# Feature products split over the rows of the array: two half-height products per half of the columns, instead of one full-height product

## The reference, cut to what matters

```python
# block 1, per batch; x is the group-normed input
S = softmax(V_s . sigmoid(prod2 + b_s))           # (N, N), spatial attention
for k in range(3):
    r = einsum('mn,bmn,bmft->bnft', cheb[k], S, x)
    out = out + einsum('bnft,fo->bnot', r, Theta[k])
sg = relu(out)
tc = conv(sg, tw, kernel 1x3 over time) + tb
y = layer_norm(relu(einsum('bnft,of->bnot', x, rw) + rb + tc))
# block 2: gate -> softmax -> top 2 of 8 experts -> gelu(x w1) * (x w3) -> w2
```

## Time and profile before

| | us |
|---|---|
| median of 3 runs | 697.05 (696.73 to 697.25) |
| the profiled execution's own time | 696.03 |
| its span | 694.0 |
| PE busy | 555.2 (80%) |
| DVE busy | 409.3 (59%) |
| ACT busy | 251.8 (36%) |
| POOL busy | 213.7 (31%) |

### The profile page before, as it was taken

How to read it: one execution, slowest core, us unless ns; L and a number is a source line. 1 busy time by engine, 2 the same in 40 slices (tenths; PEclk the granted TensorE clock), 3 DMA queues, 4 the chain that set the end, 5 groups by cost and what they waited for, 6 DMA issues and landing times. The chain is left out here.

```text
span 694.0 us, 12572 instructions
## 1 busy us (share of the span) xinstructions
PE 555.2 (80%) x2488; PEld 362.5 (52%) x2489; DVE 409.3 (59%) x1809; ACT 251.8 (36%) x619; POOL 213.7 (31%) x283
## 2 busy tenths in 40 slices
PE   0567599999999999999985225999999999999243
PEld 0233357766666666666663102666666666665122
DVE  4645236888888888988889771333333333332255
ACT  0343144345544444445442110333333333333232
POOL 5000001224333444443345440334334433443100
PEclk9989599999999999999999556999999999999655
DMA  9900000000000000000001032222222222221597
GB/s 299 421 4 1 0 1 1 0 1 32 31 30 30 31 30 30 30 23 23 27 27 55 31 106 70 77 85 83 84 85 91 78 85 87 91 83 42 164 321 240
DMA packets 36247, 52.69 MB, mean 76 GB/s; under 512 B 4606, under 2 KB 31361, under 8 KB 35969
## 3 DMA queue, kind: packets, MB, share of 16 engines
q1 hardware_dynamic: 24816, 30.86, 14.3%
q0 software_dynamic: 6480, 16.85, 6.5%
q10 hardware_dynamic: 4928, 4.72, 2.1%
HBM read 30.19 MB, written 23.14 MB: 77 GB/s over the span
## 5 line engine op out<-in xcount | busy, mean ns | idle before, releaser
L619 PE MATMUL bank<-w,xT 128*128 x284 | 135.9, 601 | 2.1 <-DVE xT L1420 2.1
L1420 DVE COPY xT<-bank 128x256 f32<-128x256 f32 x71 | 30.2, 425 | 143.8 <-PE bank L606 143.8
L975 POOL DMA_INDIRECT yrows<-xT,dest x71 | 69.4, 978 | 139.4 <-ACT xT L831 135.3
L496 PE MATMUL bank<-work 128*128 128x256 f32 x384 | 93.3, 386 | 0.0
L944 POOL DMA_INDIRECT xrows<-xtok,slot x64 | 64.3, 1005 | 81.4 <-DVEq L1315 66.7
L932 POOL TENSOR_TENSOR yg<-work,sml 128x512 f32<-128x512 f32 x16 | 18.0, 1122 | 196.3 <-DVE work L1225 193.0
L496 PEld LDWEIGHTS bank<-work 128*128 128x128 f32 x384 | 70.4, 190 | 9.0 <-issue 0.8
L634 PE MATMUL bank<-w,xT 128*128 x284 | 73.3, 380 | 1.6 <-ACT xT L836 1.6
L619 PEld LDWEIGHTS bank<-w,xT 128*128 128x128 f32 x284 | 48.8, 192 | 37.6 <-issue 37.6
L825 ACT ACTIVATE xT<-bank 128x256 f32<-128x256 f32 x71 | 27.4, 386 | 94.9 <-PE bank L619 94.9
L634 PEld LDWEIGHTS bank<-w,xT 128*128 128x128 f32 x284 | 48.5, 190 | 6.2 <-issue 2.6
(11 more groups left out here) (203 smaller groups left out, 1017.9 us busy)
## 6 DMA issues: line engine op xcount, KB each, us to landing
xT<-xrows SPq DMA_DIRECT2D x71, 129.0 KB
xT<-yrows SPq DMA_DIRECT2D x32, 256.0 KB, 3.9
xs<-x_in SPq DMA_DIRECT2D x4, 1024.0 KB, 10.8
w<-w13t_in SPq DMA_DIRECT2D x1, 4096.0 KB, 18.3
out<-xT ACTq DMA_DIRECT2D x16, 256.0 KB, 3.7
w<-w2t_in SPq DMA_DIRECT2D x1, 2048.0 KB, 22.7
yrows<-xT,dest POOLq DMA_INDIRECT x71, 2.4
xrows<-xtok,slot POOLq DMA_INDIRECT x64
```

The lines of the kernel that those rows point to most:

```text
L496: last = mm(bank[6][:, h * N:(h + 1) * N], z[:, p, c, k, h], A[:, p, c, k], start=(c == 0 and k == 0), stop=(c == C - 1 and k == K - 1))
L619: last = mm(bank[2 + q][:, :], xc[:, q, c], w13[:, e, c].rearrange("p w n -> p (w n)"), start=(c == 0), stop=(c == C - 1))
L975: pool.indirect_dma_start(yrows, bass.IndirectOffsetOnAxis(ap=dest[:, q], axis=0), yo[:, q], None, bounds_check=2 * TOKENS - 1, oob_is_err ...
L1420: V.tensor_copy(xc[:, q].rearrange("p c k -> p (c k)"), bank[q][:, 0:C * P]).then_inc(c_xc, 1)
```

## The change

One call of `features` now makes four products of 64 rows by 192 columns, where it made two of 128 rows by 384 columns. Row half r holds the time steps 4r to 4r+3 of each h. Since `thetabd` is block-diagonal, rows 0 to 63 have something only in the columns of their own four time steps, and so have rows 64 to 127: the products left out are those with blocks of zeros. Row half r of both h goes into `bank[4 + r]`, h = 0 into its first 192 columns and h = 1 into the next. ACT's two copies per call are now one per r, of 384 columns each as before, and write to `z` in runs of 64. A call now waits once for both copies of the call before it, and `b_z` is raised once per bank, after the h = 1 product.

```diff
             def features(b, p, c):

                 pe.wait_ge(s["b_xb"], done(b))
+                pe.wait_ge(s["b_zc"], (b * 4 + c * 2) + START)
                 for h in range(H):
-                    pe.wait_ge(s["b_zc"], (b * 4 + (c * H + h)) + (START - 1))
-                    mm(bank[4 + h][:, 0:K * P], xTb[:, p, h, c * P:(c + 1) * P],
-                       thetabd[:].rearrange("p k t o -> p (k t o)"), start=True, stop=True).then_inc(s["b_z"], 1)
+                    for r in range(2):
+                        rows = slice(r * P // 2, (r + 1) * P // 2)
+                        last = mm(bank[4 + r][:, h * K * P // 2:(h + 1) * K * P // 2], xTb[rows, p, h, c * P:(c + 1) * P],
+                                  thetabd[rows, :, r * TH // 2:(r + 1) * TH // 2].rearrange("p k t o -> p k (t o)"),
+                                  start=True, stop=True)
+                        if h == H - 1:
+                            last.then_inc(s["b_z"], 1)
...
             def copy_features(b, p, c):
-                for h in range(H):
-                    act.wait_ge(s["b_z"], (b * 4 + (c * H + h + 1)) + START)
-                    nc.scalar.copy(z[:, p, c, :, h], bank[4 + h][:, 0:K * P].rearrange("p (k o) -> p k o", k=K)
+                for r in range(2):
+                    act.wait_ge(s["b_z"], (b * 4 + (c * 2 + r + 1)) + START)
+                    nc.scalar.copy(z[:, p, c, :, :, r * P // 2:(r + 1) * P // 2],
+                                   bank[4 + r][:, 0:K * P].rearrange("p (h k o) -> p k h o", h=H, k=K)
                                    ).then_inc(s["b_zc"], 1)
```

## The result

The changed kernel takes 706.24 us (median of 4 runs, 704.71 to 707.76), the one before 697.15 in the same rounds: 1.0114 times as long, 95% interval 1.0084 to 1.0143. (The two medians by themselves give 1.0130.) It is slower by 1.1%, where 0.12% faster was forecast. The profiled execution took 707.76 us, with a span of 705.7.

The account below looks back on a forecast made before the run. PE was taken to bound turns -1 to 1 and DVE's chain turns 3 and later. Changes of -0.24, -0.29 and -0.29 us sum to -0.8, so 697.05 becomes 696.2 us, range 694.9 to 698.9.

Parts of the forecast that it names:

- What bounds which turn: PE sets turns -1 to 1; DVE's own chain sets turns 3 and later, with PE waiting 0.16 or 0.38 us before `prefix`.
- The halves side by side, a call of 0.86: In `features`: eight MATMULs overlap in five steps (0.81 us), paced by weight loads to 0.86, 0.43 less; chance 55%.
- The switches: Changing array shape around `features` costs 0.19 us each: one new for a c=0 call, two for c=1.
- -0.29: Forecast change of turn 1, and of turn 0, in us: -0.24 for the c=0 call and -0.05 for c=1.
- -0.8: Forecast change of turns -1 to 1 together, in us: -0.24, -0.29 and -0.29.
- The merged wait, the copies: Waiting for both copies of the call before costs 0; ACT's copies take 0 to 0.1 us more each, covered.
- The step that failed: From turn 3 on, a faster `features` only lengthens PE's wait before `prefix`, worth nothing.
- the sum: Adds the changes of turns -1 to 1 to -0.8 us, all coming through, and nothing from turn 3 on.
- my rivals: For `features` calls: full halving 695.2 us, 12%; second loads not hidden 698.5, 14%; halves one after another 699.3, 15%.
- the remainder of 4%: Chance of something outside, such as a copy that slows or a clock edge falling otherwise behind the stage.
- My sign of being wrong: If turns 3 and later change in length, the forecast is wrong, for then DVE isn't their bound.
- the gain is eaten: In `features`: once a call's eight MATMULs take over some 1.1 us, the switches eat the gain.

Follow-up runs that it names:

- run 1: Changed kernel plus three spare full-height products ahead of `prefix` in turns 3 to 14: 697.96 us against 697.19 before.
- Run 2: Kernel before, full-height products, from batch 5 on 256 (c=0) or 312 (c=1) of the 384 `features` columns: 706.99 us, ratio 1.0135.
- run 9: Changed kernel with both products of each h taken from rows 0 to 63: 705.21 us, a single execution.
- runs 3: Half-height form for batches 0 to 2 alone (made in turns -1 to 1), the old form for the rest: 697.90 us, ratio 1.0013.
- run 7: Changed kernel with three spare products in turns 3 to 14, more in turns -2, -1, 15 to 18 and ahead of the first expert tile: 692.37 us, ratio 0.9919.
- run 4: Changed kernel with a call's four products reordered, both h of row half 0 first, then both of row half 1: 705.97 us, ratio 1.0133.
- run 5: Changed kernel plus one spare full-height product ahead of `prefix` in turns 3 to 14: 705.83 us, ratio 1.0109.
- run 10: Changed kernel plus two spare full-height products ahead of `prefix` in turns 3 to 14: 701.06 us, a single execution.
- run 11: Changed kernel plus six spare products of 64 rows ahead of `prefix`, instead of three of 128 rows: 698.32 us, a single execution.

## Why the prediction was wrong

*What bounds which turn:* right. PE sets turns -1 to 1, and from turn 3 on the time saved in `features` appeared as a longer wait ahead of `prefix` (3.5 to 12.2 us).

*The halves side by side, a call of 0.86:* the time is right, its making only in part. There are four steps of 0.162 and not five; with one bare load and the switch at its end they also come to 0.86. That already holds the switch out of the call, which I had added once more for c=1.

*The switches:* mis-sized; I had put them at 0.19 each. Into a call it costs 0.09 (the six MATMULs of `graph` ahead of it take 118.62 - 117.23 = 1.39 in place of 1.30), and the exposed load behind it another 0.10 (125.28 - 123.45 = 1.83 in place of 1.73 for the next `logits`). Turn 1 gained 0.69 us where -0.29 was forecast; turns -1 to 1 together 1.9 in run 1 where -0.8 was.

*The merged wait, the copies:* right, they cost nothing: the two copies take 0.86 after as before 0.84 to 0.96, and DVE's wait for `product` in turn 1 is 1.38, where it was 1.82.

*The step that failed* stands in its first part: "a faster `features` only makes PE wait longer", and at the end of the sum: "From turn 3 on nothing." I priced PE's idle time at zero because DVE sets the pace. But PE's clock hangs on it. With 1.0 to 1.3 us ahead of `prefix` in place of 0.16 to 0.38, beside the 0.95 ahead of `tokens`, the clock fell seven times in ten turns, and at the worst place: within or just behind `tokens`, with `logits` next, and DVE does wait for these. DVE's waits for `gn_mean`, `gn_var` and `logits` grow from 2.4 to 9.0 us. Turns 4 to 13 took 8.3 us more, where the sum had nothing. Run 2 shows it without the change, run 1 by filling only the idle time. What picks the turns in which the clock falls, and why it fell in run 9 with less idle time than before, stays open. None of my rivals had this mechanism; the remainder of 4% named a clock edge, but behind the stage. The page of the profile did hold what I should have asked: the granted clock was 1.00 in every turn although PE waited over 1 us in each, and where a level holds, the question is how near its edge the kernel stands. The Trainium skill, page "TensorE: Matmul & The Clock Gate", section "Why this matters for your kernels", warns of long idle gaps between bursts of matmuls; this case shows that shorter ones can do it too: in turns 4 to 13 no gap was over 1.3 us, with five small products between the two of a turn, and they cost the clock in seven of ten turns.

*My sign of being wrong,* that turns 3 and later change in length, came true from turn 4 on: 18.4 to 19.2 us and more; turn 3 stayed, 17.90 and 17.89. But the reason that I gave for it there ("for then DVE isn't their bound") is wrong too: at the full clock DVE is their bound (run 1).

*Two slips that change nothing:* PE shows a 9 in the seventh to the twentieth slice and an 8 in the twenty-first, and DVE a 6 in the seventh; and with the prediction's own terms the gain is eaten as soon as a call's eight MATMULs take over 1.0 us, not 1.1.

## What to carry to other kernels

Time saved on TensorE where another engine sets the pace isn't worth nothing, it can be worth less than nothing: it becomes idle time, and if the granted clock falls, the products right behind the gap, for which the others wait, run at half speed. Before shortening an engine's work off the critical path, add up its idle time per turn and look at the granted clock of each stretch; if the clock stands at 1.00 with a gap in every turn, shorten only where TensorE is the bound, or give the time back as spare products into a PSUM bank that nobody reads, which is cheap to try and to size (one, two, three of them). Here each of these by itself (runs 3 and 1) only came back to the time of before; faster was only run 7, with spare products at the other gaps as well. A busy share cannot show this: PE is busy 80% before and 79% after.

## What the runs showed of the hardware

- Two f32 products of 64 rows each, on different halves of the rows and into different banks, run side by side: 0.86 us for eight MATMULs of 192 columns, 1.49 us on the same rows. Their order in the code made no difference (run 4).
- Going from 128 rows to 64 cost TensorE about 0.09 us (1.39 in place of 1.30 for six MATMULs ahead of the call), and 0.10 us on the way back (1.83 in place of 1.73 for eight behind it).
- One fall of the granted clock to 1.2 GHz (234.06 to 237.48 us in the changed kernel) cost 1.1 to 1.5 us: turns 4 to 13 were longer by 8.3 us with seven falls, by 6.8 with six (run 5) and by 2.9 with two (run 10).
- With much the same two waits in every turn of the changed kernel the clock fell at the end of seven of ten turns, 0 to 1.2 us behind the start of `tokens`. In run 4 one fall came within the second wait (174.36 us, `tokens` at 174.72).
- The sum of the idle time isn't all that counts: with 8.7 us of it the clock fell twice in run 9 and never in run 11, and with 13.0 never in the kernel before.
- The kernel before itself ran from 693.64 to 703.23 us in 19 runs beside runs 1 to 4. Single profiled spans, 696.8 for run 1 and 694.0 before, can't rank kernels that differ by 2 us; stretches of their traces can.
